# The retention state's update as eight 32-column products in PSUM, issued between state application and values

## The reference

```
x = x + 0.5 * ffn(layernorm(x))        # gate/up/down, inner width 768, weights rounded to fp8 values
x = x + attn(layernorm(x))
x = x + 0.5 * ffn(layernorm(x))

# attn: 16 heads of width 16
q, k, v = split(x @ w_qkv); q, k = xpos(q), xpos(k)
scores  = (q @ k^T) * 16**-0.5 * mask          # mask[t,s] = gamma_h**(t-s) for s <= t, else 0
y       = scores @ v
yn      = groupnorm(y per head) * gn_weight + gn_bias
out     = (silu(x @ w_g) * yn) @ w_proj
```

## Time and profile before

| what | value |
|---|---|
| median of 3 runs | 160.75 us (160.12 to 160.98) |
| span of the profiled execution, first to last instruction | 159.3 us |
| median less that span | 1.45 us |
| PE busy | 152.0 us, 95% of the span |
| DVE busy | 129.3 us, 81% |
| ACT busy | 76.4 us, 48% |
| POOL busy | 69.2 us, 43% |
| granted TensorE clock, mean | 1.000 |

### The profile page before, as it was taken

One profiled execution on the slowest core, in us unless ns is written; L12 is line 12 of the kernel. 1 busy time (PEld: TensorE's weight loads), 2 busy tenths in 40 slices (PEclk: granted clock), 3 DMA queues, 4 the chain that ended last, 5 costly groups with the idle time before them and its releaser, 6 DMA issues.

```text
span 159.3 us, 3258 instructions
## 1 busy us (share of the span) xinstructions
PE 152.0 (95%) x1115; PEld 118.9 (75%) x1115; DVE 129.3 (81%) x283; ACT 76.4 (48%) x171; POOL 69.2 (43%) x77
## 2 busy tenths in 40 slices
PE   5979899999999999999999999899899999999992
PEld 2356588789979568957786868578588888888991
DVE  0697999998877678769797999899966999756784
ACT  3467997587113151435335252536537557473310
POOL 2467244774973300545372746347599430000000
PEclk9999999999999999999999999999999999999999
DMA  4999302804000000000000000000000000001104
GB/s 141 312 364 321 131 0 74 327 3 132 0 4 0 0 0 4 0 0 0 4 2 4 2 0 4 0 0 4 4 0 4 0 0 0 0 0 52 51 33 134
DMA packets 7008, 8.41 MB, mean 53 GB/s; under 512 B 448, under 2 KB 5712, under 8 KB 6992
## 3 DMA queue, kind: packets, MB, share of 16 engines
q1 hardware_dynamic: 6816, 8.13, 15.3%
q10 hardware_dynamic: 176, 0.07, 0.3%
HBM read 7.15 MB, written 1.05 MB: 51 GB/s over the span
## 4 chain that ended last, share of the span: by engine, by line
PE 85%; DVE 5%; DMA 3%; ACT 2%; issue 1%; POOL 1%; SPq 1%; ACTq 0%
PE bank L1154 26%; PE bank L1182 13%; PE bank L1210 9%; PE bank L1254 5%; PE bank L1278 5%; PE bank L1334 5%; PE bank L1222 5%; PE bank L1225 4%; DMA raw<-in_L_ffn_up_w 3%; PE bank L1291 2%; PE bank L1237 2%; PE bank L1270 2%; PE bank L1324 1%; PE bank L1108 1%; PE bank L1311 1%
## 5 line engine op out<-in xcount | busy, mean ns | idle before, releaser
L1154 PE MATMUL bank<-hh,up_r 128*128 128x512 f32 x92 | 25.5, 400 | 0.1
L1154 PE MATMUL bank<-hh,gate_r 128*128 128x512 f32 x92 | 25.6, 401 | 0.0
L1182 PE MATMUL bank<-down_r,fhi 128*128 128x256 f32 x96 | 24.2, 290 | 0.0
L337 POOL TENSOR_TENSOR grstd<-gve,neg_half 128x16 f32<-128x16 f32 x8 | 23.3, 2915 | 0.8 <-POOL gve L333 0.2
L1182 PE MATMUL bank<-down_r,flo 128*128 128x256 f32 x96 | 23.4, 282 | 0.0
L794 DVE TENSOR_TENSOR sc<-bank,msk 128x512 f32<-128x512 f32 x32 | 20.7, 682 | 0.1
L453 ACT ACTIVATE gact<-bank,vec 128x512 f32<-128x512 f32 x24 | 16.3, 685 | 8.5 <-PE bank L1154 7.6
L1154 PEld LDWEIGHTS bank<-hh,up_r 128*128 128x128 f32 x92 | 16.8, 188 | 4.2 <-issue 0.5
L461 ACT ACTIVATE fhi<-fuse 128x512 fp32r<-128x512 f32 x24 | 14.6, 625 | 10.8 <-DVE fuse L737 10.8
L1154 PEld LDWEIGHTS bank<-hh,gate_r 128*128 128x128 f32 x92 | 16.9, 189 | 3.8 <-ACT gate_r L402 0.2
L1182 PEld LDWEIGHTS bank<-down_r,fhi 128*128 128x128 f32 x96 | 18.1, 188 | 1.0 <-issue 0.6
(11 more groups left out here) (89 smaller groups left out, 288.3 us busy)
## 6 DMA issues: line engine op xcount, KB each, us to landing
raw<-in_rotation SPq DMA_DIRECT2D x1, 1536.0 KB, 7.2
out<-xt SPq DMA_DIRECT2D x8, 128.0 KB, 2.0
raw<-in_L_ffn_down_w SPq DMA_DIRECT2D x2, 384.0 KB, 8.0
wqkv<-in_L_attn_w_qkv SPq DMA_DIRECT2D x1, 768.0 KB, 9.0
xt<-in_L_attn_x SPq DMA_DIRECT2D x2, 256.0 KB, 3.5
xt<-in_L_attn_x SPq DMA_DIRECT2D x1, 512.0 KB, 6.4
raw<-in_rotation SPq DMA_DIRECT2D x1, 512.0 KB, 3.6
raw<-in_L_ffn_gate_w SPq DMA_DIRECT2D x1, 384.0 KB, 6.9
```

What stands on the lines that cost most here:

```text
L337: pool.tensor_tensor(grstd[:, c % 2], gve[:, :], neg_half[:, :], ALU.pow).then_inc(grstd_done, 1)
L1154: mm = pe.matmul(dst[:, :], wr[m][:, k * I + i * P:k * I + (i + 1) * P], half[:, k, g % NG, :], start=(k == 0 and half is hhi), stop=(k == ...
L1182: mm = pe.matmul(downs[d][:, 0:C], half[:, g % NG, i, t * P:(t + 1) * P], wr["down"][:, i * C:(i + 1) * C], start=(i == 0 and half is fhi) ...
```

## The change

- The product k^T v is made in pairs of heads: eight products, each with 32 columns of k as the stationary operand and the matching 32 columns of v moving, in four column groups of the array. Only the 32x32 blocks that hold a head's own part (two heads each) are made: 128x64 in PSUM instead of 128x256.
- That result lies in bank 2, columns 0 to 63, where `project_vg` writes v. So the update waits until `copy_v(c+1)` has emptied the bank (`sg_done`), and `project_vg(c)` waits for `mask_kv(c-2)`.
- `update_state(c)` is called inside `values(c)`, behind the state application and ahead of scores times v.
- `mask_kv(c)` reads each of the 64 columns four times to widen the result to 128x256, and stands behind `mask_scores(c, 3)`.
- `copy_v(2)` and `copy_v(7)` stand one place earlier on ACT.

```diff
-        b_y, b_kv, b_qk, b_vg = bank[0][:, 0:C], bank[0][:, C:2 * C], bank[1], bank[2]
+        b_y, b_qk, b_vg = bank[0][:, 0:C], bank[1], bank[2]
+        b_kv = bank[2][:, 0:KC * 2 * D]
...
             copy_qk(2)
+            copy_v(2)
             copy_y(1)
-            copy_v(2)
...
-                dve.tensor_tensor(dst, b_kv.rearrange("p (k d) -> p k d", k=KC),
-                                  own.unsqueeze(1).to_broadcast([P, KC, P]), ALU.mult).then_inc(kvm_done, 1)
+                dve.tensor_tensor(dst.rearrange("p k (r w) -> p k r w", r=HG),
+                                  b_kv.rearrange("p (k w) -> p k w", k=KC).unsqueeze(2).to_broadcast([P, KC, HG, 2 * D]),
+                                  own.rearrange("p (r w) -> p r w", r=HG).unsqueeze(1).to_broadcast([P, KC, HG, 2 * D]),
+                                  ALU.mult).then_inc(kvm_done, 1)
...
                     pe.wait_ge(sg_done, c)
+                if c >= 2:
+                    pe.wait_ge(kvm_done, c - 1)
...
                 pe.wait_ge(v_done, c + 1)
-                if c < NT - 1:
-                    pe.wait_ge(kvm_done, c + 1)
                 if c >= 1:
                     pe.wait_ge(yT_done, c)
                     pe.wait_ge(qT_copied, c + 1)
+                    pe.wait_ge(kvm_done, 1)
...
+                if c < NT - 1:
+                    update_state(c)
...
                 pe.wait_ge(rot_done, 2 * (c + 1))
-                pe.wait_ge(v_done, c + 1)
-                if c == 0:
-                    pe.wait_ge(hlo_done, KC * NG)
-                else:
-                    pe.wait_ge(yT_done, c)
-                    pe.wait_ge(kvm_done, c)
+                pe.wait_ge(sg_done, c + 2)
                 for k in range(KC):
-                    mm = pe.matmul(b_kv[:, k * P:(k + 1) * P], rot[:, c % 2, C + k * P:C + (k + 1) * P],
-                                   v_own[c % 2][:, 4 * k:4 * k + 4], start=True, stop=True)
+                    for r in range(HG):
+                        a = k * HG + r
+                        mm = pe.matmul(b_kv[r * 2 * D:(r + 1) * 2 * D, k * 2 * D:(k + 1) * 2 * D],
+                                       rot[:, c % 2, C + a * 2 * D:C + (a + 1) * 2 * D], v_own[c % 2][:, a],
+                                       start=True, stop=True)
                 mm.then_inc(kv_done, 1)
```

More of the change, by code:

```diff
@@ L605, in _ @@
             copy_qk(7)
+            copy_v(7)
             affine(4)
-            copy_v(7)
             copy_y(6)
@@ L940, in _ @@
             mask_scores(0, 3)
+            rotate_parts(2)
             mask_kv(0)
-            rotate_parts(2)
             rotate(2)
@@ L947, in _ @@
             mask_scores(1, 2)
-            mask_kv(1)
             group_mean(0)
             mask_scores(1, 3)
+            mask_kv(1)
             tile_stats(12)
@@ L962, in _ @@
                 group_norm(c - 2)
-                mask_kv(c)
                 mask_scores(c, 2)
                 mask_scores(c, 3)
+                mask_kv(c)
                 norm_stats(NT + c + 3, NT + c + 4)
@@ L974, in _ @@
             tile_stats(16)
-            mask_kv(5)
             rotate(6)
@@ L980, in _ @@
             mask_scores(5, 3)
+            mask_kv(5)
             tile_stats(17)
@@ L994, in _ @@
             add_proj(3)
-            mask_kv(6)
             group_norm(4)
             mask_scores(6, 3)
+            mask_kv(6)
             tile_stats(19)
@@ L1392, in _ @@
             turn_h2(2)
-            update_state(0)
             turn_qk(1)
@@ L1402, in _ @@
             turn_h2(3)
-            update_state(1)
             turn_y(0)
@@ L1413, in _ @@
                 turn_h2(c + 2)
-                update_state(c)
                 turn_qk(c + 1)
@@ L1420, in _ @@
                 scores(c + 1)
-            update_state(5)
             project_vg(6)
@@ L1430, in _ @@
             scores(6)
-            update_state(6)
             project_out(3)
```

## The result

| | before | after |
|---|---|---|
| median us | 160.60 (4 runs, 160.12 to 160.98) | **169.51** (4 runs, 169.01 to 170.35) |
| span of the profiled execution | 159.3 | 167.2 |
| ratio, 95% interval | | 1.056 (1.053 to 1.059) |

The change makes the kernel 5.6% slower; 169.1 was predicted.

A forecast was written before the change was run, and what follows sets the result against it. Each loop block was bound by PE and an equally long chain through the group norm at once. Terms of 8.4 us took the span from 159.3 to 167.7; with 1.45 outside it, the median was 169.1 us, range 166.0 to 171.2.

The forecast's parts named there:

- tiles 0 and 1: Updates there wait for ACT's copies, the gate copy of tile 1 first, so values end later: +0.9 us by tile 1.
- tiles 2 to 4: Loop blocks lengthen to 9.9 us, then 10.2, against 8.89 and 8.99; values end +3.7 us late by then, +2.8 in the sum.
- tile 5: DVE work queued behind mask_kv(4) delays turn_h2(7) on PE: 11.0 us against 9.40, +1.6.
- tile 6: mask_kv(5) holds back eight DVE steps up to the group variance of tile 4: 9.15 us against 6.49, +2.7.
- after: Second-FFN norm tiles stand behind mask_kv(6), so turn_h ends later relative to values(6): +0.4 us.
- The ring: Loop: DVE's mask waits for PE's product, delaying group mean, variance and norm, for which PE waits: 10.2 us a block.
- Rival 1: The mask's wait is absorbed in DVE's 1.05 us idle time: 160.6 us, or 158.5 with X = 0.13; 6 in 100.
- Rival 2: Only part bites: the loop pays, but tiles 5 and 6 find slack: 164.9 us; 14 in 100.
- Rival 3: The 32-column products don't overlap, each pass costing 0.11 like an old 128x128 one: 179 us; 4 in 100.
- X: PE time of one update's 16 passes of 32 columns: 0.43 us, between 0.13 and 0.53, entering the sum seven times.
- The 0.28 for a restart: Extra PE time for a group started after a wait, 0.50 against 0.22; good to some 1 us over about ten.
- The mask's widening: Fourfold read in DVE's mask costs nothing, at most 0.1 us per block, adding up to 0.7 us in all.

The follow-up runs named there:

- late mask: Changed kernel, mask behind statistics and gate product in blocks 2 to 4, behind the gate product in tile 5, POOL's root before its state sum: 162.72 us, ratio 1.013.
- the old form in the new place: Changed kernel with the product as two 128x128 products and the plain mask, all places and orders as changed: 171.36 us, ratio 1.067.
- the two halves: Changed kernel with the late mask's edits in the loop alone (165.02 us, ratio 1.027), or in tile 5 alone (167.12 us, ratio 1.040).
- the combined kernel: The late mask, also late for tiles 1, 5, 6, POOL's roots before state sums, copy_v(1) before copy_qk(1), square before y copy: 160.59 us, ratio 1.000.
- doubled products: Changed kernel with each update's eight products made twice into the same place, 16 more passes per update: 171.02 us, ratio 1.061.

## Why the prediction was right, step by step

The steps are read off PE's timelines, from where the group behind `values` starts (67.94, 95.51, 104.91 and 111.40 before; 68.21, 98.43, 109.45 and 118.49 after). The profiled execution after was 0.38 ahead before the first update: the last `rotate(0)` on DVE stands at 56.23 there and at 56.61 before. The first row takes that back.

| step | predicted us | measured us |
|---|---|---|
| tiles 0 and 1 | +0.9 | +0.65 (0.27 + 0.38) |
| tiles 2 to 4 | +2.8 | +2.65 (30.22 against 27.57) |
| tile 5 | +1.6 | +1.6 (11.02 against 9.40) |
| tile 6 | +2.7 | +2.55 (9.04 against 6.49) |
| after | +0.4 | +0.8 (48.7 against 47.9) |
| sum | 8.4 | 8.25; 7.9 between the spans |

**The ring was the cause.** Its signs are all there: 2.01 of idle time ahead of the mask in blocks 2 to 4 and 2.47 in block 5, none ahead of the variance, PE's longest waits ahead of `turn_h2(7)` and `project_out(3)`. The prediction asked for a period of 10.2; it is 10.16 and 10.25, though this close only because misses in its terms cancel (below). The late mask shows the cause, and the old form in the new place excludes the form. Rival 1, the wait absorbed, fell as said: 2.01 is twice the idle time. Rival 2, tiles 5 and 6 free, fell too: the two halves give 4.5 and 2.4. Rival 3, products as dear as the old passes, fell by the 0.14.

**The price X was mis-sized, and the ring hid it.** X was 0.43 of PE time for 16 passes. They hold PE for 0.14, at the prediction's lower end of 0.13; by that the forecast would have been 2.0 lower. What the ring counts, though, is the time until DVE may start, and from the product's start to the mask it is 0.40 to 0.41 (76.83 to 77.23, 86.98 to 87.39), against the 0.48 of X and hand-over. The estimate that the prediction worked out from the Trainium skill (TensorEngine Tiling (Array Packing), Instruction Overhead), 0.40 for the 16 passes, is three times what the trace shows. What is removed was mis-sized too: 0.45 is the old update in tiles 0 to 2, while it takes 0.51 in blocks 3 and 4 and 0.55 in tiles 5 and 6, 3.5 us in all instead of 3.15.

**The ring's terms missed both ways, and the misses cancel.** From mask to variance the forecast has 2.60 (its 2.65 less the hand-over of 0.05), and it took 2.78, because the gate product (L844) took 0.62 in place of the 0.41 to 0.43 of before: POOL's sum of the state runs beside it, from 77.73 to 78.45. Elsewhere the group norm of tile 6 met the same (above). The chain of work, in which the prediction read PE's terms, shows the opposite miss:

```profile
87.05 0.31 PE bank L1294 x16
...
87.39 0.43 DVE kvm L806
```

Product and hand-over are 0.34 there, against 0.48. The ring's other parts held: variance to norm 3.74 and 3.84 (3.8), norm to product 3.30 (83.75 to 87.05; 3.31). The 0.28 for a restart is read across two views: on PE's timeline of before `turn_gn` starts at 82.72, 0.06 behind the norm's end, and `project_qk` at 82.99, so a restart costs 0.11, and the other 0.17 is the lag by which the chain dates a group later; in the ring that lag is counted once, and the sum holds. So the ring is right, and that its length came out within 0.1 us is in part luck.

**The median was met with luck as well.** The span was forecast at 167.7 and is 167.2, 0.5 less. The prediction added 1.45 for what lies outside the span; in the profiled execution it is 2.0 (169.23 less 167.2). The two misses nearly make up for each other.

**The mask's widening** was costed at nothing, and the mask takes 0.42 as before. The wait for the gate copy in tiles 0 and 1 was seen (0.31 and 0.39 ahead of the products of tiles 0 and 1) and a little smaller than priced; the price's own terms add up to 68.88 instead of 68.95, which is +0.9 either way. The upper end of the forecast's range adds up to 171.5 and not 171.2.

**After tile 6** twice the priced 0.4: the last norm tile on DVE starts at 120.62, and `turn_h`, which ran as one group of 1.04 in the earlier trace rows, is cut in two, its last pair at 121.15. It gives way to the next group 2.94 after `values(6)` (118.49 to 121.43), before after 2.37 (111.40 to 113.77); that is 0.57, and the other 0.2 stay open. With the last mask behind three of the four norm tiles, in the combined kernel, `turn_h` is one group again.

## What to carry to other kernels

An engine that seems to have room, DVE at 81% here, has none at the place where an instruction waits for a product made later: price the wait by what is queued behind it, and follow that until it comes back to the engine that makes the product; if it does, the wait is paid in every turn of the loop. When a producer moves later in one program, move its consumer behind all work that doesn't need it: that gave back 6.8 of 8.9 us. And a smaller tile form gained most next to a group of the same form (0.14 us against 0.54), and hardly anything between full-array groups (0.05).

## What the runs showed of the hardware

- **32-column passes are cheap beside their own kind.** 16 passes took 0.14 us ahead of `values`, 32 took 0.27: some 8.5 ns a pass. Between full-array groups the same 16 cost about 0.40 in all, 0.26 and 0.14 more in the groups around them.
- **DVE and POOL collide on short instructions.** In the changed kernel the gate product takes 0.62 beside POOL's sum of the state. With POOL's order changed the collision moves to the norm tile, as the timelines of DVE and POOL show:

```profile
78.96 0.41 DVE L844 TENSOR_TENSOR go<-ga,sg 128x256 f32<-128x256 f32 x1
...
80.13 0.81 DVE L709 TENSOR_SCALAR h<-x,mv,rstd 128x256 f32<-128x256 f32 x1
...
80.06 0.73 POOL L346 TENSOR_TENSOR state<-state,kvm 128x256 f32<-128x256 f32 x1
```

  The gate product is back at 0.41, and the norm tile, 0.41 otherwise, takes 0.81. It does so beside POOL in the kernel before as well (0.82 at 51.12). In all these cases, the group norm's above too, the DVE instruction started inside POOL's and ended 0.15 to 0.29 behind it. Not every DVE instruction is held up: a rotation product (L775, one operand in PSUM), started at 109.34 in the changed kernel inside POOL's sum (109.17 to 109.90), took 0.67, as it does alone. The Trainium skill (SBUF — State Buffer, SBUF: two separate sides) describes a port pair that the two engines share as an exclusive lock, which whoever comes first holds for the whole instruction, and names DVE instructions with two inputs in SBUF among those that need it. Gate product and group norm have two such inputs, the rotation product has one; these cases fit that. For the norm tile, which reads one tensor in SBUF, no run here shows why it is held up.
- **The clock fell behind a wait, but not each time.** In two of four executions with doubled products, and in two of four with the old form, the mean granted clock was 0.988 or 0.989. In the profiled one of each it fell behind `project_out(3)`, for part of the time from 2.4 GHz to 1.2 (means of 0.84 and 0.73 in the windows above; 0.94 and 0.63 with the old form). PE had waited 1.62 and 1.49 us ahead of that group and was busy for 2.30 and 1.97 of the 4 us of the first window. The executions at the lower clock took some 2.5 us longer than those at full clock with the doubled products, and 1.2 with the old form. The changed kernel waits as long there (1.64), and its profiled execution kept the full clock, so that the wait is the cause is not shown, and what decides is left open.
